# Mask moments in two fused VectorE passes, and the residual kept in memory as whole images

## What is computed

```python
# layer 0, on the group-normalised input
sumX = maximum(x.sum((2, 3)), 1e-9)
mu_x = maximum(round((ix * x).sum((2, 3)) / sumX), 1)      # ix, iy = 1 .. 28
mu_y = maximum(round((iy * x).sum((2, 3)) / sumX), 1)
m = 1 - (abs(posX - lin[mu_x - 1]) + abs(posY - lin[mu_y - 1])) * mask_weight
m = where(filt == 1, maximum(m, -1), 1)
x' = x + conv3x3(relu(x * m), weight) + bias               # the residual add, per image

# layer 1, on the group-normalised x', token by token (784 tokens, chunks of 16)
q, k, v = rope(xn @ q_w.T), rope(xn @ k_w.T), xn @ v_w.T
for each of the 49 chunks, per image and head:             # a scan over W1, b1
    grad = ln_l2_bwd(xk @ W1 + b1, xv - xk)
    out  = xq + ln(xq @ W1 - (eta * tril(xq @ xk.T)) @ grad + b1 - tril(eta) @ grad)
    W1  -= (eta_last * xk).T @ grad;  b1 -= (eta_last * grad).sum
y = x' + ln(out) @ o_w.T
```

## Time and profile before

| | us |
|---|---|
| median of three runs | 1995.46 (1990.15 to 1995.93) |
| the profiled execution's own time | 1991.81 |
| its span in the profile | 1989.7 |
| PE busy | 1620.6 (81%) |
| DVE busy | 1579.8 (79%) |
| POOL busy | 1315.9 (66%) |
| ACT busy | 991.3 (50%) |
| DMA: the SP queue's packets | 1390640 packets, 51.0% of 16 engines' span |
| DMA: the ACT queue's packets | 259504 packets, 10.7% |
| TensorE clock granted, mean | 0.643 of full speed |

### The profile page before, as it was taken

The page is one execution under the profiler, slowest core; times in us unless marked ns, Lnnn a source line. Parts: engine busy times, 40 slices in busy tenths (PEclk is TensorE's granted clock), DMA queues, the critical chain, the costliest instruction groups (busy, mean ns, idle before and its releaser), DMA issues.

```text
span 1989.7 us, 82066 instructions
## 1 busy us (share of the span) xinstructions
PE 1620.6 (81%) x33520; PEld 1206.9 (61%) x33520; DVE 1579.8 (79%) x3721; ACT 991.3 (50%) x2358; POOL 1315.9 (66%) x1479
## 2 busy tenths in 40 slices
PE   1886978922798889888888888888888898888886
PEld 1443544511676667767667667667676676676674
DVE  6999997704788788888888887887888887888864
ACT  2223545443455555555555555555555555555553
POOL 1244535365687787777777777777777777777763
PEclk9997999965555655555555556655566555655555
DMA  6058696963465665675665665665656656666554
GB/s 238 1 30 45 97 97 68 81 148 69 52 76 68 71 80 69 74 78 67 73 79 68 73 73 70 76 72 68 80 65 73 79 68 72 73 70 76 67 61 49
DMA packets 1650518, 148.80 MB, mean 75 GB/s; under 512 B 1630176, under 2 KB 1643744, under 8 KB 1650144
## 3 DMA queue, kind: packets, MB, share of 16 engines
q1 hardware_dynamic: 1390640, 117.87, 51.0%
q10 hardware_dynamic: 259504, 25.70, 10.7%
HBM read 40.71 MB, written 38.54 MB: 40 GB/s over the span
## 4 chain that ended last, share of the span: by engine, by line
SPq 24%; PE 16%; DVE 15%; DMA 10%; issue 7%; ACT 3%; DVEq 0%; POOL 0%; ACTq 0%; POOLq 0%
SPq L477 16%; DMA kqk<-work 8%; SPq L493 7%; PE p_kt L1624 6%; PE p_x L1668 4%; DVE work L1303 2%; DMA late<-work 2%; DVE work L1270 2%; DVE work L1294 2%; PE p_m L1653 2%; DVE work L1363 1%; PE p_x L1659 1%; DVE work L1385 1%; DVE zs L1350 1%; DVE m L1357 1%
## 5 line engine op out<-in xcount | busy, mean ns | idle before, releaser
L795 ACT ACTIVATE work<-p_kt 128x512 f16<-128x512 f32 x196 | 149.1, 761 | 213.7 <-PE p_kt L1624 212.9
L1624 PEld LDWEIGHTS p_kt<-fold,kqk 128*128 128x128 f16 x6272 | 185.0, 104 | 97.2 <-ACT work L795 46.1
L1624 PE MATMUL p_kt<-fold,kqk 128*128 128x16 f16 x6272 | 200.6, 175 | 52.8 <-DMA kqk<-work 45.0
L1597 PE MATMUL p_j<-wa,work 128*128 128x512 f16 x196 | 119.5, 610 | 146.9 <-DVE work L1270 102.2
L621 POOL TENSOR_TENSOR work<-work,rope_s 128x256 f32<-128x256 f32 x196 | 161.5, 844 | 83.8 <-DVE work L1270 83.8
L592 POOL TENSOR_TENSOR work<-work,g 128x256 f32<-128x256 f32 x98 | 71.8, 732 | 201.7 <-DVE work L1341 198.8
L1303 DVE TENSOR_TENSOR work<-work 128x256 f16<-128x256 f32 x196 | 164.3, 893 | 15.8 <-ACT work L782 15.8
L1532 PE MATMUL p_j<-work 128*128 128x392 f16 x864 | 157.7, 344 | 23.3 <-DVE work L1117 20.7
L1668 PEld LDWEIGHTS p_y<-w,late 128*128 128x128 f16 x4704 | 145.7, 103 | 17.9 <-issue 8.5
L1668 PEld LDWEIGHTS p_x<-w,late 128*128 128x128 f16 x4704 | 149.0, 105 | 12.3
L1597 PEld LDWEIGHTS p_j<-wa,work 128*128 128x128 f16 x196 | 24.9, 127 | 207.4 <-issue 176.6
(11 more groups left out here) (173 smaller groups left out, 4397.4 us busy)
## 6 DMA issues: line engine op xcount, KB each, us to landing
kqk<-work SPq DMA_DIRECT2D x392, 64.0 KB, 4.7
late<-work SPq DMA_DIRECT2D x392, 64.0 KB, 3.8
late<-work SPq DMA_DIRECT2D x392, 32.0 KB, 2.6
out_y<-work ACTq DMA_DIRECT2D x49, 256.0 KB, 6.8
x_scratch<-late SPq DMA_DIRECT2D x24, 392.0 KB, 11.8
xs_scratch<-work SPq DMA_DIRECT2D x24, 392.0 KB, 6.5
work<-x_scratch ACTq DMA_DIRECT2D x49, 192.0 KB, 3.6
work<-xs_scratch SPq DMA_DIRECT2D x48, 192.0 KB, 2.8
```

Of the source, the lines that this page charges most:

```text
L795: return act.activation(kqt16[:, o, g:g + GP, :, :, :].rearrange("p g h t a -> p g a (h t)"), p_kt[:, :].rearrange("p (g a n) -> p g a n", ...
L1597: pe.matmul(p_j[k][:, 0:4 * C], tokens(s, k, 0), wa16[:, :], start=True, stop=False, skip_group_check=True)
L1624: mm = pe.matmul(p_kt[:, at:at + CS], part_of(g + k, h, a), fold16[:, :], start=True, stop=True)
```

## The change

In words:

- **Mask moments.** The row and column sums, their weighting and the reductions are replaced by two passes over the image, each of which multiplies with a broadcast ramp and gives its sum as an accumulator output (`mask_rows`, `mask_cols`). The products go to `mk`, which is rewritten later. The total is an accumulator output of `normalise` on ACT.
- **Rounding.** The ramp has the rounding constant added once (`ramp_r`), so that the second rounding step goes.
- **Magnitude and parts** move from DVE to ACT (`mask_parts`, three activations). ACT's order has them after the group-norm root, and `relu` of image b+2 now comes after `scaled`.
- **Start.** The group norm of images 0 and 1 is done by itself first; that of images 2 to 7 follows during image 0. The statistics of images 2 to 7 come between the steps of the first two masks.
- **Residual.** x' of every group is stored with one transfer of eight whole images, and `xr_load` is one transfer of 32 images in 4096 pieces of 64 bytes.

The diff, cut to its core:

```diff
-        x2_d = nc.dram_tensor("x2_scratch", (NCH, C, FRONT, CS), F32, kind="Internal").ap()
-        x2_t = nc.dram_tensor("x2_scratch_tail", (GB, C, HW), F32, kind="Internal").ap()
+        x2_d = nc.dram_tensor("x2_scratch", (B, C, HW), F32, kind="Internal").ap()
...
             def x2_store(q):
...
-                if q == NG - 1:
-                    sp.dma_start(x2_t.rearrange("b c n -> c b n"), xres[:, at:at + GB, :]).then_inc(s_x2[q], 16)
-                else:
-                    for k in range(GB):
-                        sp.dma_start(x2_d[:, :, GB * q + k, :].rearrange("n c t -> c n t"),
-                                     xres[:, at + k, :].rearrange("c (n t) -> c n t", t=CS)).then_inc(s_x2[q], 16)
+                sp.dma_start(x2_d[GB * q:GB * (q + 1)].rearrange("b c n -> c b n"), xres[:, at:at + GB, :]).then_inc(s_x2[q], 16)
...
-                act.dma_start(xr[:, c % 2, 0:FRONT, :].rearrange("c b t -> c (b t)"),
-                             x2_d[c].rearrange("c b t -> c (b t)")).then_inc(xr_landed.sem(c), 16)
-                act.dma_start(xr[:, c % 2, FRONT:B, :], x2_t[:, :, CS * c:CS * (c + 1)].rearrange("b c n -> c b n")).then_inc(xr_landed.sem(c), 16)
+                act.dma_start(xr[:, c % 2, :, :], x2_d[:, :, CS * c:CS * (c + 1)].rearrange("b c n -> c b n")).then_inc(xr_landed.sem(c), 16)
...
                 act.activation(gx[:, b % 4, :], image_of(b), ACT.Identity, bias=gshift[:, b:b + 1],
-                               scale=gscale[:, b:b + 1]).then_inc(cv_g.sem, 1)
+                               scale=gscale[:, b:b + 1], accum_out=tot[:, b % 4:b % 4 + 1]).then_inc(cv_g.sem, 1)
...
+            def mask_parts(b):
+                p = b % 2
+                act.wait_ge(cv_v.sem, cv_v.count("dist", b))
+                flat = ab[:, p, :, :].rearrange("c a i -> c (a i)")
+                act.activation(flat, flat, ACT.Abs).then_inc(cv_m.sem, 1)
+                act.wait_ge(cv_m.sem, cv_m.count("absd", b))
+                act.activation(ab[:, p, 0, :], ab[:, p, 0, :], ACT.Identity, bias=eps_s[:, 4:5], scale=mwn[:, 0:1]).then_inc(cv_m.sem, 1)
+                act.activation(ab[:, p, 1, :], ab[:, p, 1, :], ACT.Copy, scale=mwn[:, 0:1]).then_inc(cv_m.sem, 1)
...
                 if i == 1 and q > 0:
-                    gn_root(2 * q, GB * (q - 1), GB)
+                    gn_root(2 * q + 1, GB * (q - 1), GB)
+                if b + 2 < B:
+                    mask_parts(b + 2)
+                for k in scaled_at(b):
+                    scaled(k)
                 if b + 2 < B:
                     relu(b + 2)
-                for k in scaled_at(b):
-                    scaled(k)
...
-            def mask_sums(b):
...
-                dve.tensor_reduce(rc[:, 0, :], img2, AX.X, ALU.add).then_inc(cv_v.sem, 1)
-                dve.tensor_reduce(rc[:, 1, :], img2.rearrange("c i j -> c j i"), AX.X, ALU.add).then_inc(cv_v.sem, 1)
+            def mask_rows(b):
...
+                dve.scalar_tensor_tensor(out=prod, in0=img2, scalar=1.0,
+                                         in1=ramp_s[:, 0, :].rearrange("c (i o) -> c i o", o=1).to_broadcast([C, H, W]),
+                                         op0=ALU.mult, op1=ALU.mult, accum_out=cen[:, 0:1]).then_inc(cv_v.sem, 1)
...
+            stats_first(0)
+            stats_first(1)
+            gn_centre(0, 0, 2)
+            gn_scale(0, 0, 2)
+            mask_point(0)
+            stats_first(2)
             dve.wait_ge(cw.sem, cw.count("high", 0))
...
+            masked(0)
+            mask_point(1)
+            stats_first(3)
+            stats_first(4)
+            masked(1)
+            stats_first(5)
+            stats_first(6)
+            stats_first(7)
+            gn_centre(1, 2, GB - 2)
+            gn_scale(1, 2, GB - 2)
```

More of the change, by code:

```diff
@@ L269, in program @@
         cv_s = steps("conv_scalar", "relu high")
[L270 removed]
+        cv_v = steps("conv_mask_vector", "rows cols floor inv ratio magic dist masked")
+        cv_m = steps("conv_mask_scalar", "absd row_part col_part")
         cv_p = steps("conv_pool", "mask lo")
@@ L1090, in _, with stats_first @@
             dve.tensor_tensor(mwn, mwn, vec[:, V_MW:V_MW + 1], ALU.mult).then_inc(s_mwn, 1)
-            dve.wait_ge(s_mwn, 2)
-            for b in range(GB):
+            dve.tensor_scalar(ramp_r, ramp_s, ROUND, None, ALU.add).then_inc(s_mwn, 1)
+            dve.wait_ge(s_mwn, 3)
+            def stats_first(b):
                 if b % 2 == 0:
@@ L1100, in _, with mask_point @@
                 stats_kept(b)
-            gn_centre(0, 0, GB)
-            gn_scale(0, 0, GB)
-            for b in range(2):
-                mask_sums(b)
-                mask_weigh(b)
-                mask_moment(b)
+            def mask_point(b):
+                mask_rows(b)
+                mask_cols(b)
                 mask_floor(b)
@@ L1543, in _ @@
             pe.wait_ge(s_first, 48)
-            pe.wait_ge(bn1.sem, bn1.count("aggr", GB - 1))
-            gn_mean(0, 0, GB)
-            gn_var(0, 0, GB)
+            pe.wait_ge(bn1.sem, bn1.count("aggr", 1))
+            gn_mean(0, 0, 2)
+            gn_var(0, 0, 2)
             pe.wait_ge(cw.sem, cw.count("low", 0))
```

147 lines of the change are left out of this document (65 added, 82 removed).

## The result

| | before | change |
|---|---|---|
| median | 1995.7 us (1990.15 to 1996.08) | 2021.91 us (2019.44 to 2025.82, four runs) |
| ratio, 95% interval | | 1.0147 [1.0126, 1.0168] |
| span in the profile | 1989.7 | 2021.6 |
| PE busy | 1620.6 | 1622.0 |
| DVE busy | 1579.8 | 1524.5 |

The change is slower by 1.5%. DVE has 55 us less to do, and the kernel loses 26 us. The two profiled spans differ by 31.9 us: the convolution ends 9.8 us earlier, the passage gives 2.1 more, the 48 turns of the scan lose 42.1 and the tail behind the last chunk 1.7. So the scan decides it, as forecast, and the convolution gave a quarter of what was forecast.

A forecast was written before the change was run, and what follows sets the result against it. It saw the scan bound by a loop through SP and DMA, and DVE slower than PE in the convolution; 1991.8 less 41, 1 and 7, plus 59, is 2001.8, median 2005 us, range 1956 to 2040.

The forecast's parts named there:

- the passage: Stretch between convolution and scan: single-transfer x' stores free SP, so group 2's last images pass POOL earlier; 7 us gained.
- the sign: Whole kernel: slower, median 2005 us, +0.5%; chances 0.51 slower, 0.17 same, 0.32 faster.
- The load's pieces must come out of the spreads' time: Scan: the residual load shares DMA engines with the spreads and delays `kq_spread`; 1.2 us a chunk, 59 us in all.
- the price of the pieces: Scan: 2944 more pieces per chunk at 0.64 us per thousand, at most 1.9 us, in 29 of 40 chunks.
- `relu` behind `scaled` costs nothing while the stores keep up: ACT's order in the convolution: the moved `relu` adds no time, provided image stores keep up; size nothing.
- rival 3: Convolution doesn't follow: ACT's cover lost at turns, or accumulator outputs 0.3 or more; 20 us less gained, 2025; chance 0.1.
- the size of the convolution's gain: Convolution stage: PE becomes the pace, and shorter waits and fewer slow matmuls together give 41 us.
- Group-norm waits, 48.6 to 21: Convolution: PE's waits before group-norm matmuls shrink, 28 us gained; the wait at the `kqk` clear goes from 16.3 to 12.
- Short waits for `relu_low` and DVE's lag, 6 less: Convolution: PE's short waits for `relu_low` and DVE's remaining lag shrink, giving 6 us.
- DVE's rhythm: Convolution: DVE's images with statistics go from 10.2 us to 8.2 to 8.9, under PE's 9.17.
- its rule on two inputs against POOL: Convolution: two-input fused DVE passes and POOL lock each other out; `relu_low` starts up to one pass later, inside the cover.
- rival 4: Passage stores: SP's queue stays full, image stores alone issuing at 5.3 us each; the 7 us don't come, 2012; chance 0.05.

The follow-up runs named there:

- e4_load_big: The change with the residual load of the same bytes in 128 pieces of 2048 bytes instead of 4096 of 64; median 1971.34 us, ratio 0.9897.
- e3_relu_first: The change with ACT's `relu` put ahead of `scaled` again, nothing else; median 2009.63 us, ratio 1.0098.
- e6_mask_relu_first: The change without its residual part (stores and loads as before) and with `relu` ahead of `scaled`; median 1981.13 us, ratio 0.9964.
- e5_load_later: The change with the residual load moved in ACT's order from ahead of the chunk's first `z_square` to behind its first `kt_copy`; median 1943.97 us, ratio 0.9783.

## Why the prediction was right and wrong

**Right: the sign and its reason.** "The load's pieces must come out of the spreads' time" holds. The chunk is 31.16 us for 31.4 forecast; the eight issues are stretched to 11.4, and `kq_spread` lands 0.9 us later on the mean. PE's waits for it rose by 13 us only; PE's stops inside its matmuls, some 20 us more, were not foreseen, and whether they cost anything of their own is open. The Trainium skill (page "DMA: Bandwidth & Descriptors", section "Issuing engines are not separate DMA queues") was on this side, and the trace agrees, with 7215 packets of one queue among 8311 of the other. What it leaves open is the place: beside `kq_spread` the same transfer costs 1.75 us a chunk more than beside `m_spread` (31.16 against 29.41), beside `turned_spread` 1.1 more (30.63 against 29.50, both with `relu` first).

**Mis-sized: the price of the pieces.** The step was 0.64 us per thousand, from the pace of SP's own transfers, in 29 of 40 chunks: 1.2 us. Measured are 0.88 us a chunk, 0.30 per thousand, and 0.26 to 0.32 in `e4_load_big`. The error: 0.64 is what a piece takes when its queue runs alone and one issue follows the other. Pieces added beside another queue's cost half of that here. The second source of the price (3.25 us for 5248 pieces) put all of the stretch on pieces, where `e4_load_big` still has issues of 9.80 us (10.0 on the mean). The scan was to lose 59 us and lost 42.1, 17 in the change's favour.

**Wrong: the step "`relu` behind `scaled` costs nothing while the stores keep up".** Its condition did hold: where ACT waited, SP's queue was free, and the store had been issued as soon as POOL had finished its image. But a store lands 6.0 to 9.4 us after its issue, POOL's `scaled_low` stands behind `relu_low`, and so `relu` behind `scaled` makes the next stores late as well. ACT waits for the DMA ten times, 32.1 us in all (before, by the same view, 5 times and 18.0 us, with the `relu` of that place ahead of it). `e3_relu_first` gives 10 to 12 us back in the change, `e6_mask_relu_first` 20 in the mask part alone. It is a share of rival 3 (cover on ACT lost), at another place and with a larger price than the turns had there.

**Wrong: the size of the convolution's gain,** 41 us forecast and 9.8 measured. This is the term that put the sum off. By its parts:

- Group-norm waits, 48.6 to 21: they fell to 25.2. Nearly right; the clear kept 16.4 instead of 12.
- Short waits for `relu_low` and DVE's lag, 6 less: without the one at the start the waits are 20.0 us (31.3 less 11.3), against 4.4 before without the one in front of image 2. 16 more, not 6 less: for the most part the step above.
- Fewer slow first groups after long waits, 7: hardly came. PE still has waits of 16.4, 7.9 and 7.7 us, and its matmuls are slow behind them as before (10.98 for 54 at 163.91, 9.33 otherwise). From 99 us on, the slow groups together take 7.9 us more than others of their size, and before they took 8.5.

From image 2 to the last matmul, PE waits 22.3 us for the group norms and waited 46.5 (the 25.2 and 48.6 hold waits behind the last matmul too), and 20.0 for `relu_low` where it waited 4.4: 8.5 us less in all. Image 2 starts 0.3 us earlier, and PE works 1.0 us less. That is the 9.8, and the early start of images 0 and 1 gives nothing.

Behind this lies a forecast of DVE's rhythm, 8.2 to 8.9 us. It counted one operation that waits for POOL, beside `relu_low`, and that came: the ratio step takes 0.86 to 1.21 us there and 0.21 to 0.23 with POOL idle. It left out `scaled_low`, beside which the rounding step takes 1.4 to 1.8 us for 0.15. So the forecast holds in images 1 and 2, where no `scaled_low` runs (8.6 and 8.9 in the change), and fails where it does (9.9 with one in the image, 11.4 and 11.8 with two, in `e3_relu_first`); before, the latter two images took 11.4 and 12.0, so they gained next to nothing. The Trainium skill has such a lock (page "SBUF — State Buffer", section "Who interferes with whom": a port pair that VectorE and GpSimd share is locked for the whole instruction, and the form of the VectorE instruction decides whether it takes part). The prediction used its rule on two inputs against POOL, and there the trace agrees: `relu_low` starts under the second fused pass in 24 images and takes 1.72 to 2.23 us in them, against 1.62 to 1.64 beside the one-input reduction of before. The Trainium skill limits that rule to a GpSimd instruction that reads SBUF (same page and section); the 18.69 us of the earlier trace rows are another case, since that step has one tensor input and the clear reads nothing. The trace shows the lock against DVE too, 1.80 us for an operation of 0.15. That the held operations explain all of the remaining gap was read from the trace and not tried by itself.

**Right: the start.** First matmul at 30.13 for 29.5 forecast; image 2 at 62.99 for 62.5; no gain.

**Wrong in part: the passage,** 7 us forecast, 2 measured. SP is free of x' as forecast, but ACT waits for a store's landing in front of each of the last images: the last image of group 2 passes POOL 9.6 us after PE's end and not 4. The outcome is rival 4's, and its reason is not: "image stores alone issue at 5.3 us each (42.55 for eight)" reads a merged row as a full queue. Five of these eight took 0.36 us to issue, and SP was idle between them; only the first ones had stood behind the stores of x'. In the change, too, it is the landing (6.1 to 6.3 us for most) and not the queue.

The sum again: 2001.8 was forecast for the profiled execution, and it took 2023.39, 21.6 more. The convolution and the start made 32 of it (42 less 9.8), the passage 5, the tail behind the last chunk 1.7; the scan's overrated price took 17 off. That the median, 2021.91, lies only 17 us above the forecast is thus partly luck: two errors stand against each other. It also lies near rival 3's 2025, but with a cheaper scan, so that rival's sum did not come true either.

## What to carry to other kernels

A transfer on a queue of its own is not free, and its price depends more on where it falls than on what it is: find out which transfer the loop waits for, and place bulk traffic in small pieces beside one that it doesn't. Here the move of one line brought 3.6% in the change and 2.0% in the kernel before, and one place further on lost three quarters of the gain. When work is moved to an engine with idle time, look at what that engine's order will wait for behind it (here `relu` behind a `scaled` that waits for a transfer), and look whether GpSimd works beside the small VectorE operations: an engine that is made faster may only wait elsewhere.

## What was not expected of the hardware

- Small pieces cost less beside another queue's: 0.26 to 0.32 us per thousand 64-byte pieces, half of the 0.64 that one queue alone shows. Beside a transfer that nobody waits for they cost nothing that shows.
- POOL operations on whole images, a clear without input included, hold up some small VectorE operations until they end. The two-element rounding step takes 1.80 us for 0.15 beside an image operation. The ratio step takes 0.21 to 0.23 with POOL idle, 0.86 to 1.21 beside `relu_low`, 3.45 beside `relu_low` and a clear of 2.65, and 18.69 beside a clear of 20.58. A one-element step of the same kind (0.15) is never held, in 24 of 24 images of the change. A clear cut in pieces holds DVE up by the same sum.
- The accumulator output costs little: a read of 0.08 us on VectorE and 0.19 on ScalarE; the VectorE pass takes as long as one without it (0.97).
- PE can stop inside a group of matmuls for up to 1.9 us while the profile shows nothing that it waits for; these stops came and went with the load's pieces (35.7 us in the change between 700 and 1900 us, 15.3 before, 1.9 in `e5_load_later`). Their cause is open.
